# Perceiver block with cross attention, a state-space layer and routed experts: Silu gates in one step of ScalarE, taps in three steps, time-step row by a product, and five late units moved behind the attention

## The reference, cut to what matters

```python
x = x + xattn(ctx_1024, layernorm(x), ...)     # 8 batches, 64 latents, 1024 + 64 rows, 16 heads of 64
x = x + ssm(layernorm(x), ...)                 # below
x = x + experts(layernorm(x), ...)             # 8 experts, gather by top_idx, scatter-add

def ssm(x, ...):                               # x: 8 sequences of 64 tokens, 256 wide; inner width 512
    xn = norm(x); xz = xn @ W_in; xc, z = split(xz)
    xc = silu(sum(pad(xc)[:, k:k+L] * conv_w[:, k] for k in range(4)) + conv_b)
    dbc = xc @ x_proj_w                        # 33 columns: dt, 16 of B, 16 of C
    dt = softplus(dbc[:, :1] * dt_w + dt_b)
    h_t = exp(dt_t * A) * h_(t-1) + dt_t * B_t * x_t      # 16 states n for each channel
    y = sum_n(h * C) + xc * D
    return (y * silu(z)) @ W_out + residual
```

## Time and profile before

| what | us |
| --- | --- |
| median of 3 runs (lowest, highest) | 867.31 (865.99, 867.49) |
| the profiled execution | 868.61 |
| its span | 866.9 |
| busy PE, DVE, ACT, POOL | 751.0, 530.5, 411.0, 426.4 |
| mean granted clock of TensorE | 0.938 of full speed |

### The profile page before, as it was taken

The page is one execution under the profiler, slowest core; times in us unless marked ns, Lnnn a source line. Parts: engine busy times, 40 slices in busy tenths (PEclk is TensorE's granted clock), DMA queues, the critical chain, the costliest instruction groups (busy, mean ns, idle before and its releaser), DMA issues. The chain is left out here.

```text
span 866.9 us, 14301 instructions
## 1 busy us (share of the span) xinstructions
PE 751.0 (87%) x5373; PEld 687.1 (79%) x5373; DVE 530.5 (61%) x1100; ACT 411.0 (47%) x1119; POOL 426.4 (49%) x398
## 2 busy tenths in 40 slices
PE   4869999999989999997789999968887736879996
PEld 3459999999989889997789999968877624448895
DVE  5146566557586866978686778785676536960112
ACT  2424554544445556554465655543645405734341
POOL 2805304402532776765668857754878844710000
PEclk9969999999999999998899999988999856899998
DMA  9540020010002002200110021000011106501720
GB/s 315 219 109 1 2 61 14 1 61 14 1 7 79 24 13 74 32 13 7 65 38 17 10 74 33 16 3 14 22 19 28 28 3 230 208 0 49 252 88 26
DMA packets 49271, 49.25 MB, mean 57 GB/s; under 512 B 18404, under 2 KB 44080, under 8 KB 48048
## 3 DMA queue, kind: packets, MB, share of 16 engines
q1 hardware_dynamic: 49200, 48.31, 18.4%
HBM read 43.91 MB, written 4.26 MB: 56 GB/s over the span
## 5 line engine op out<-in xcount | busy, mean ns | idle before, releaser
L1233 ACT ACTIVATE pt_hi<-psum 128x512 fp32r<-128x512 f32 (+1 forms) x192 | 87.4, 490 | 199.0 <-PE psum L1573 151.2
L1590 PE MATMUL psum<-kvn_hi,pt_hi 128*128 128x256 f32 x512 | 150.7, 294 | 2.1 <-DVE pt_hi L837 2.1
L1590 PE MATMUL psum<-kvn_hi,pt_lo 128*128 128x256 f32 x512 | 145.1, 283 | 0.0
L1590 PE MATMUL psum<-kvn_lo,pt_hi 128*128 128x256 f32 x512 | 145.0, 283 | 0.0
L939 DVE TENSOR_REDUCE rowmax<-psum 128x1 f32<-128x728 f32 x64 | 58.6, 915 | 95.6 <-PE psum L1557 95.3
L1557 PE MATMUL psum<-kvt_hi,qk_hi 128*128 128x364 f32 (+1 forms) x384 | 95.8, 360 | 23.6 <-DVE kvt_lo L798 12.7
L1590 PEld LDWEIGHTS psum<-kvn_hi,pt_hi 128*128 128x128 f32 x512 | 98.2, 192 | 2.4 <-DVE pt_hi L837 2.4
L1590 PEld LDWEIGHTS psum<-kvn_lo,pt_hi 128*128 128x128 f32 x512 | 98.3, 192 | 0.1
L1590 PEld LDWEIGHTS psum<-kvn_hi,pt_lo 128*128 128x128 f32 x512 | 98.0, 191 | 0.0
L611 POOL TENSOR_TENSOR work<-work,bc 128x512 f32<-128x512 f32 x48 | 62.5, 1303 | 55.7 <-DVE work L925 55.7
L840 DVE TENSOR_TENSOR pt_lo<-psum,pt_hi 128x512 fp32r<-128x512 f32 x128 | 81.9, 682 | 12.7 <-ACT pt_hi L1233 12.7
(11 more groups left out here) (236 smaller groups left out, 1532.6 us busy)
## 6 DMA issues: line engine op xcount, KB each, us to landing
w<-in_L_ffn_W_dram SPq DMA_DIRECT2D x16, 1024.0 KB, 7.5
ctx_nat<-in_ctx_dram SPq DMA_DIRECT2D x8, 1024.0 KB, 5.2
bc<-dbc_keep SPq DMA_DIRECT2D x48, 128.0 KB, 4.7
q_keep<-q_t SPq DMA_DIRECT2D x1, 2048.0 KB, 8.5
q_cur<-q_keep SPq DMA_DIRECT2D x14, 128.0 KB, 3.0
wk_nat<-in_L_xattn_Wkv_dram SPq DMA_DIRECT2D x1, 1024.0 KB, 6.0
wq_sb<-in_L_xattn_Wq_dram SPq DMA_DIRECT2D x1, 1024.0 KB, 12.2
wv<-in_L_xattn_Wkv_dram SPq DMA_DIRECT2D x1, 1024.0 KB, 14.5
```

Of the source, the lines that this page charges most:

```text
L1233: act.activation(pt_hi[u][:, t0:t1, :], where[:, 0:(t1 - t0) * P].rearrange("p (t m) -> p t m", m=P), ACT.Copy)\
L1590: pe.matmul(PV, w[u][:, j, :], x_[slot][:, j, :], start=(j == 0 and w is pt_hi and x_ is kvn_hi), stop=False)
```

## The change

What it does, by step of a pair (r):

- **Gates.** `exp_conv`, `exp_z`, `plus_one`, `invert`, `gate_conv` and `gate_z` go. `gates` on ACT at r = 5 does both with the function Silu, straight from PSUM for z, behind the exponentials of the step; the compiler puts a table load before the first and one behind the second. The z product moves to the end of r = 4, for all three pairs. `zs` has two buffers, `gate` and `dt_row` are gone.
- **Taps.** Tile 0 at r = 2, tiles 1 and 2 at r = 3, tile 3 at r = 4.
- **Time-step row.** `x_proj` at r = 6, its row 0 spread over 128 partitions by a PE product (`spread`) at the end of that step into the bank `TP[1]`; `time_lin` at r = 6 reads it there, PE waits for it (`v_dl`) at r = 7 before its transposes. `softplus` and `time_steps` at 7, `time_x` at 7, `skip_x` one instruction at 8, the first unit at 8, `times_gate` and `w_out` at 24, `mixed` at 25.
- **Units.** Pair 2 has three units in two steps; the last five go behind the attention, into the front of pair 3 (three) and its open loop (two). `times_gate` of pair 2 comes after the fourth drive of the open loop, its `w_out` after the fifth sum, its `mixed` in the seventh turn.
- **Small.** `token_norm` on POOL at r = 0; `y_skip` and `skip_x` as one instruction with a broadcast operand.

```diff
+        FIRST_UNIT = 2 * HP + 3 + 8
+        AFTER = HP * B + 2
         def unit_step(u):
             t, n = divmod(u, NS)
             if t < INLINE - 1:
-                return 2 * HP * t + 26 + n
-            return 2 * HP * t + 26 + n // 2
+                return 2 * HP * t + FIRST_UNIT + n
+            return min(2 * HP * t + FIRST_UNIT + 2 * n // 3, AFTER)
...
+            for u in units_at[AFTER][:3]:
+                load_rows(u)
             sp.wait_ge(s_woe, B // 2)
             sp.dma_start(comb[:], combine_w[0:T, :].rearrange("(t p) e -> p t e", p=P)).then_inc(ld_comb, 16)
             sp.dma_start(b1_rows[:], b1.rearrange("e (f p) -> (e f) p", p=P)).then_inc(ld_comb, 16)
+            for u in units_at[AFTER][3:]:
+                load_rows(u)
             sp.wait_ge(r_cnt, 1)
             sp.dma_start(b2_sb[:], b2).then_inc(ld_b2, 16)
             load_expert(0, 0)
-            sp.wait_ge(v_acc, NS * INLINE)
+            sp.wait_ge(v_acc, NS * (INLINE - 1))
             sp.wait_ge(v_dbs, INLINE + 1)
             sp.dma_start(dbc_keep[INLINE % 2], dbc[:]).then_inc(st_dbc, 16)
...
-                for r in (2, 3):
+                for r, tiles in ((2, (0,)), (3, (1, 2)), (4, (3,))):
                     t = pair_at(g, r)
                     if t is not None:
-                        taps(t, r - 2)
-                t = pair_at(g, 5)
+                        taps(t, tiles)
+                t = pair_at(g, 6)
                 if t is not None:
                     time_lin(t)
+                t = pair_at(g, 7)
+                if t is not None:
+                    time_steps(t)
...
+            def gates(t):
+                act.wait_ge(v_tap, DT * TAPS * (t + 1))
+                act.wait_ge(v_z, t + 1)
...
+                act.activation(zs[t % 2][:], MB.rearrange("p (d m) -> p d m", m=P), ACT.Silu).then_inc(v_zc, 1)
+                act.activation(xc[:], conv[:], ACT.Silu).then_inc(v_xc, 1)
+                act.preload_act_table_set("natural_log_exp_and_others")
...
+                t = pair_at(g, 6)
+                if t is not None:
+                    pe.wait_ge(v_dbs, t + 1)
+                    pe.wait_ge(s_lB, count(now[0], now[2]))
+                    spread(TP[1][:, 0:P], 0).then_inc(v_dt, 1)
+                t = pair_at(g, 24)
                 if t is not None and t < INLINE - 1:
                     pe.wait_ge(v_y, t + 1)
-                    pe.wait_ge(s_mlo, misc_count(b, 3))
-                    w_out(gate, MB[:, 0:C]).then_inc(v_yo, 1)
+                    pe.wait_ge(s_mlo, misc_count(b + 1, 0) if b + 1 < B else MISC * B)
+                    w_out(zs[t % 2], MB[:, 0:C]).then_inc(v_yo, 1)
...
             for n in range(NS):
                 scan_open(n)
-                if n == 2:
+                if n < 2:
+                    scan_unit(left[3 + n])
+                if n == 6:
                     mixed(INLINE - 1, psum[:, WB, 0:C])
```

More of the change, by code:

```diff
@@ L97, in perceiver_kernel @@
         conv = sb(live, "conv", [P, DT, P])
-        gate = sb(live, "gate", [P, DT, P])
         xc = sb(live, "xc", [P, DT, P])
-        zs = sb(live, "zs", [P, DT, P])
+        zs = [sb(live, f"zs{i}", [P, DT, P]) for i in range(2)]
         dts = sb(live, "dts", [P, DT, P])
@@ L729, in _ @@
             step(B, 1, False)
-            pool.wait_ge(s_woe, TT)
+            first, *rest = units_at[AFTER - 1]
+            close_unit(first)
             token_norm(INLINE)
-            for u in units_at[HP * B + 1]:
+            for u in rest:
                 close_unit(u)
-            times_gate(INLINE - 1)
+            left = units_at[AFTER]
+            open_unit(left[0])
             link(pool.memset(zero[:], 0.0))
@@ L875, in turned_in, with taps @@
                 last.then_inc(v_xte, 1)
-            def taps(t, part):
-                dve.wait_ge(v_pad, t + 1)
-                if t >= 1 and part == 0:
-                    dve.wait_ge(v_dts, t)
-                first = 2 * (2 * t + part) * TAPS
+            def taps(t, tiles):
+                if tiles[0] == 0:
+                    dve.wait_ge(v_pad, t + 1)
+                    if t >= 1:
+                        dve.wait_ge(v_dts, t)
+                made = TAPS * (DT * t + tiles[0])
                 for k in range(TAPS):
-                    for j in range(2):
-                        d, n = 2 * part + j, first + 2 * k + j
+                    for j, d in enumerate(tiles):
                         o = conv[:, d, :].rearrange("p (s l) -> p s l", l=L)
@@ L1333, in middle @@
                 if t is not None:
+                    gates(t)
+                t = pair_at(g, 6)
+                if t is not None:
                     keep_rows(t)
+                t = pair_at(g, 7)
+                if t is not None:
+                    softplus(t)
                 for u in units_at.get(g, ())[1:]:
@@ L1654, in w_out, with spread @@
                 return last
+            def spread(where, r):
+                return pe.matmul(where, ident[0:NX, r:r + 1].to_broadcast((NX, P)), dbc[:], start=True, stop=True)
             def before_turns(b, hp):
@@ L1792, in _ @@
             list_slots()
-            def spread(where, r):
-                return pe.matmul(where, ident[0:NX, r:r + 1].to_broadcast((NX, P)), dbc[:], start=True, stop=True)
             pe.wait_ge(v_dbs, INLINE + 1)
@@ L1811, in _ @@
             spread_out(1)
-            pe.wait_ge(v_xte, INLINE + 2)
-            pe.wait_ge(v_y, INLINE)
-            w_out(gate, psum[:, WB, 0:C]).then_inc(v_yo, 1)
             def sum_states(n):
@@ L1857, in _ @@
                 sum_states(n)
+                if n == 4:
+                    pe.wait_ge(v_y, INLINE)
+                    w_out(zs[(INLINE - 1) % 2], psum[:, WB, 0:C]).then_inc(v_yo, 1)
                 if n < E + 3:
```

226 lines of the change are left out of this document (96 added, 130 removed).

## The result

| | before | changed |
| --- | --- | --- |
| median of 9 runs (lowest, highest), us | 866.78 (860.98, 869.42) | 859.13 (855.29, 862.62) |
| span of the profiled execution, us | 866.9 | 854.3 |
| mean granted clock of TensorE | 0.938 | 0.945 |

The ratio is 0.9913, 95% interval [0.9895, 0.9932]: 0.87% faster. The forecast was 868.7, no change that could be told. The time lies inside the range of 851 to 880, but by luck: the gain has a cause that neither the forecast nor any of its rivals has.

The account below looks back on a forecast made before the run. It took the attention as bound by PE's time plus stalls, 59 us in idle time and low clock before the drain. Terms -2.8 + 4.6 - 14.1 - 4.5 + 9.0 + 9.2 = +1.4 gave 868.7 us by median, range 851 to 880.

Parts of the forecast that it names:

- pair 0: Steps 19 to 34: gate chain goes and half the idle time with it, against a new z-gate wait; -2.8 us.
- pair 1: Steps 38 and 40 to 42 shorter; 39 longer by taps beside POOL, 43 and 44 by late time_x; +4.6 us.
- pair 2 and drain: Fewer units in steps 59 to 63, steps 61 to 63 at 7.9 us each; -14.1, and drain waits mostly go, -4.5.
- front of pair 3: Taps slowed beside POOL, unit 12's scan and close delay the weights, store queues behind them; +9.0 us.
- open loop: Two closes and the gate before drive 4, two more scans, w_out among the sums; +9.2 us.
- The first: Rival: POOL's ctx_low falls ahead of the taps in steps 39 and 55, 10.3 us a step; -13.4, 855.3; chance 0.36.
- The second: Rival: steps 61 to 63 keep 5/6 of their 11.3 us as scans wait behind POOL's opens; 878.1; chance 0.21.
- the table switch: Rival: a switch in the attention costs 1.4 us beyond its 1.28 us load; +4.2, 872.9; chance 0.03.
- The fourth: Rival: the store in pair 3's front does not queue behind the weights; -8, 860.7; chance 0.06.

Follow-up runs that it names:

- counts_new: The kernel before with only the changed kernel's two prologue wait counts (misc_hi on ACT, misc_lo on DVE); 858.37 us, ratio 0.9926.
- counts_old: The changed kernel with the two old prologue wait counts put back; 865.75 us, ratio 1.0001 to the kernel before.
- b_again: The kernel before run once more, nothing edited; 867.36 us, ratio 1.0015.
- gate_first: The changed kernel with POOL's times_gate ahead of the opens in its step; 859.74 us.
- store_first: The changed kernel with the store of pair 3's 33 rows and the broadcast loads issued before the first expert's weights and unit 15's rows; 853.49 us.
- combo4: The changed kernel with all 16 units of pair 2 in steps 59 to 65, taps in 1, 1, 2 tiles and the store first; 848.11 us.

## Why the forecast was wrong, step by step

**The step that failed is one that isn't there.** The sum began at pair 0. The prologue and batch 0 (114.8 of the 866.9 us) have no term, and the two lines of the diff that change the counts of their waits are not named. It put this part at nothing without a reason, and the runs show -7 to -8 us in its place: by medians counts_new lies 8.1 us under the kernel before, and counts_old 6.6 over the changed kernel. That is all of the 0.87%. The clean test of the other terms is a pair of profiles with the same counts, b_again and counts_old. b_again, cut close to the starts of steps 19, 35 and 51, at pair 3's statistics, first drive and end of loop:

```profile
207.25:359.12 151.87, 145.38 (x1168) 139.94 (x1168) 111.04 (x247) 81.34 (x221) 82.82 (x78) 1.00 0.12 32
359.12:526.31 167.19, 150.88 (x1176) 144.87 (x1176) 127.18 (x256) 89.11 (x249) 114.71 (x102) 0.97 0.13 33
526.31:698.72 172.41, 141.72 (x1048) 132.50 (x1046) 117.58 (x198) 84.66 (x249) 122.19 (x98) 0.93 0.09 17
698.72:732.13 33.41, 18.63 (x111) 14.79 (x111) 18.68 (x37) 11.61 (x28) 16.83 (x22) 0.60 0.36 107
732.13:769.65 37.52, 29.23 (x97) 13.96 (x96) 29.36 (x35) 22.22 (x67) 20.01 (x16) 0.87 0.45 159
```

counts_old, the same cuts:

```profile
207.88:355.79 147.91, 145.69 (x1172) 140.27 (x1168) 102.18 (x244) 82.14 (x218) 76.35 (x68) 1.00 0.11 32
355.79:525.72 169.93, 153.80 (x1180) 146.56 (x1176) 125.59 (x254) 90.96 (x250) 110.78 (x95) 0.96 0.12 32
525.72:681.80 156.08, 139.22 (x1050) 130.75 (x1046) 108.10 (x192) 83.66 (x238) 100.91 (x81) 0.96 0.08 16
681.80:727.14 45.34, 15.88 (x103) 12.65 (x103) 27.64 (x40) 16.74 (x44) 30.30 (x27) 0.60 0.34 98
727.14:772.48 45.34, 32.45 (x104) 16.19 (x104) 31.75 (x37) 22.63 (x67) 26.97 (x21) 0.83 0.35 125
```

| part | forecast | measured |
| --- | --- | --- |
| pair 0 | -2.8 | -4.0 |
| pair 1 | +4.6 | +2.7 |
| pair 2 and drain | -18.6 | -16.3 |
| front of pair 3 | +9.0 | +11.9 |
| open loop | +9.2 | +7.8 |
| experts | 0 | -0.9 |
| behind step 8 | +1.4 | +1.3 |

The single terms are off by up to 2.9 us and cancel; that their sum comes out within 0.1 us is luck. The prediction's narrower range of 862 to 876 does not follow from the bounds that it names (5.6 to 10 for the front, 4 to 10 for the loop, 3 us on the attention), which give 857 to 874.

- **Pair 0.** Right in kind. PE's wait for the z gate is 0.7 us (1.2 forecast).
- **Pair 1.** Right in kind: the maxima 8.5 and 8.7 us into steps 39 and 55 (8.9 forecast), PE's wait of 4.56 us in step 43 (4.8 forecast), step 38 -2.7 in the changed kernel's first profile as forecast. The reason for step 43 was half: its wait hangs on the low half behind the scan as well (gate_first).
- **Pair 2.** Steps 61 and 62 at 7.88 us (7.9 forecast) and step 54 3.1 shorter; step 55 grew by 2.8 and step 59 by 2.1.
- **Front.** Right in kind: the store issued 27.7 us behind the drain (28 forecast), and the twelve taps took 7.08 us beside POOL, for the 4.24 of the earlier trace rows and three taps at 1.35 for 0.35. Mis-sized was the landing: 10.05 us after the store's issue and not 7, 11.0 after the issue of the weights (696.14) and not 8. These 3 us are about what the front is over its term.
- **Loop.** Scan 4 started 14.9 us after the first drive (15.6 forecast).
- **The rivals.** The first asked for 10.3 us in steps 39 and 55; they took 15.4 to 17.3. The second asked for the old length of steps 61 to 63; 61 and 62 were short. For the table switch the trace has no cost beyond the load itself: each of the six `ACT_TABLE_LOAD` of the pairs and the two in the front takes 1.28 us, starts within 0.02 us behind the instruction before it, and the next one starts within 0.03 us behind it. The drain of 1.38 us, which the Trainium skill ("ScalarE: Activation LUTs", What ACT_TABLE_LOAD costs) adds to each switch, is not seen there. The fourth was wrong too: the store did queue, as store_first shows. None of them was the gain that came, so that what the prediction has right of the outcome, the chance of 0.45 for faster and the wide range, is right by luck.

## What to carry to other kernels

Go through a diff line by line until every changed line has a term, even if the term is zero, and lay the terms over the whole span: a part of the profile without a term is a hole. In a profile, compare the releaser behind each idle time with what the instruction reads; where they differ, the wait is on a count, a queue or a shared buffer. Find out which before taking it away: the two high counts here were free, while `w_out` behind `qk_lo` (gate_first) guards the bank that both use. When two engines slow each other, a product that is moved to start sooner pays for whatever it now runs beside, so look at both the place that it leaves and the one that it goes to.

## What had not been expected of the hardware

- An idle time of PE of 6.60 us in front of its first logits cost more than itself. Step 0 started 4.6 us later in b_again than in counts_new, and by step 8 the distance was 10.0. The windows of steps 0 to 7, b_again and then counts_new, have the same idle time of PE, 5.7 us; the 5.4 between them are busy time at a lower granted clock, all of it in steps 0 to 2 (25.9 us for 20.5):

```profile
45.18:113.81 68.63, 62.89 (x445) 60.85 (x445) 36.06 (x93) 29.19 (x76) 20.91 (x23) 0.90 0.17 41
40.56:103.77 63.21, 57.47 (x446) 55.43 (x446) 36.06 (x93) 29.19 (x76) 20.90 (x23) 1.00 0.24 64
```

- A step of the attention can take one of two lengths: step 39, with the same instructions, 15.4 us in the profiles of the changed kernel and of gate_late and 17.3 in the others. In the short one the maxima start 8.45 us into the step, in the long one 8.72, and there PE idles 3.1 us ahead of its turns, which it does not in the short one. Why it falls on the one or the other was not tried.
- The start of step 8 varies by 4 us between profiles whose code is the same up to there (103.8 to 108.1). It comes from the start of step 0 (39.4 to 41.1) and from steps 0 to 2 (20.5 to 24.3 us), while steps 3 to 7 take 42.7 us and steps 8 to 18 take 93.64 us in every profile. Some of the 7 us between the fastest and slowest runs of a kernel may lie there, but not all: see combo4.
